# First attention: scores as three products of rounded parts, the query factor moved into the exponential's scale

## The reference

```python
q = rms_norm(einsum('btd,ndh->btnh', x, q_kernel), q_norm_scale)    # 16 heads of 128
k = rms_norm(einsum('bsd,kdh->bskh', x, kv_kernel[0]), k_norm_scale) # 8 heads of 128
q, k = apply_rope(q, positions), apply_rope(k, positions)
logits = einsum('btkgh,bskh->bkgts', q * ATTN_SCALE, k)  # each key head serves two query heads
probs = softmax(where((j <= i) & (i - j < 128), logits, min))
out = einsum(probs, v) @ out_kernel
```

## Time and profile before

| | |
|---|---|
| median of 3 runs | 1593.5 us (1591.81 to 1593.52) |
| profiled execution, own time | 1587.25 us |
| span of its trace | 1585.4 us |
| busy: PE, DVE, ACT, POOL | 93%, 68%, 56%, 25% |
| first attention | the first 656 us or so of the span |
| mean granted TensorE clock | 0.976 of full speed |

### The profile page before, as it was taken

How to read it: one execution, slowest core, us unless ns; L and a number is a source line. 1 busy time by engine, 2 the same in 40 slices (tenths; PEclk the granted TensorE clock), 3 DMA queues, 4 the chain that set the end, 5 groups by cost and what they waited for, 6 DMA issues and landing times.

```text
span 1585.4 us, 24036 instructions
## 1 busy us (share of the span) xinstructions
PE 1478.0 (93%) x7582; PEld 1095.0 (69%) x7582; DVE 1085.6 (68%) x2404; ACT 882.6 (56%) x2052; POOL 403.2 (25%) x473
## 2 busy tenths in 40 slices
PE   4899999999998999799999999999879999999898
PEld 3788788878887888667777777777644444444476
DVE  6898699859976998377555455455438676767654
ACT  4777677757785777444332332332236565756556
POOL 4666566566655665200000000000000000000000
PEclk9999999999999999899999999999969899999999
DMA  6000000000000000233000000000030000000001
GB/s 236 1 1 1 1 1 1 1 3 1 1 1 3 1 1 1 66 91 90 20 1 1 0 0 0 0 0 0 2 135 1 1 1 0 0 0 0 1 14 40
DMA packets 15767, 28.54 MB, mean 18 GB/s; under 512 B 2000, under 2 KB 10064, under 8 KB 15024
## 3 DMA queue, kind: packets, MB, share of 16 engines
q1 hardware_dynamic: 15264, 26.51, 4.9%
q0 software_dynamic: 400, 0.78, 0.3%
HBM read 25.96 MB, written 2.10 MB: 18 GB/s over the span
## 4 chain that ended last, share of the span: by engine, by line
PE 73%; DVE 10%; issue 6%; POOL 5%; ACT 4%; DMA 1%; DVEq 0%; SPq 0%; ACTq 0%; POOLq 0%
PE ps L1126 13%; PE ps L1128 13%; PE ps L1127 13%; PE ps L1396 5%; PE ps L1179 5%; PE ps L1455 4%; PE ps L1225 4%; PE ps L1240 2%; PE ps L1377 2%; POOL rope L388 2%; PE ps L1523 2%; PE ps L1206 2%; DVE ssum L528 1%; PE ps L1281 1%; PE ps L1409 1%
## 5 line engine op out<-in xcount | busy, mean ns | idle before, releaser
L360 POOL TENSOR_TENSOR ln_rs<-ln_ve,minus_half 128x4 f32<-128x4 f32 x16 | 17.4, 1085 | 887.5 <-DVE ln_ve L424 887.5
L710 DVE TENSOR_REDUCE nm<-ps 128x1 f32<-128x512 f32 x256 | 168.3, 687 | 70.2 <-PE ps L1396 68.4
L1126 PE MATMUL ps<-xnT_lo,w1moe_hi 128*128 128x512 f32 x400 | 177.4, 444 | 2.4 <-DVE w2moe_lo L665 2.2
L1044 ACT ACTIVATE pT<-ps 128x512 f32<-128x512 f32 x256 | 143.5, 601 | 62.6 <-PE ps L1409 60.2
L960 ACT ACTIVATE moe_act_hi<-sg 128x512 fp32r<-128x512 f32 x100 | 63.3, 633 | 190.6 <-DVE sg L642 190.6
L1127 PE MATMUL ps<-xnT_hi,w1moe_lo 128*128 128x512 f32 x400 | 160.5, 401 | 0.0
L1128 PE MATMUL ps<-xnT_hi,w1moe_hi 128*128 128x512 f32 x400 | 159.9, 400 | 0.0
L388 POOL TENSOR_TENSOR rope<-rope 128x384 f32<-128x384 f32 x128 | 144.2, 1127 | 0.0
L632 DVE TENSOR_TENSOR sg<-ps,sg 128x512 f32<-128x512 f32 x100 | 69.1, 691 | 96.0 <-ACT sg L980 96.0
L892 ACT ACTIVATE raw<-ps 128x512 f32<-128x512 f32 x128 | 76.4, 597 | 99.3 <-PE ps L1128 97.0
L912 ACT ACTIVATE prob<-ps,nmax 128x256 f32<-128x256 f32 (+1 forms) x256 | 113.2, 457 | 30.8 <-DVE nmax L503 30.7
(11 more groups left out here) (204 smaller groups left out, 3747.3 us busy)
## 6 DMA issues: line engine op xcount, KB each, us to landing
yT<-in_w1moe SPq DMA_DIRECT2D x25, 256.0 KB, 2.6
encT<-in_wqkv SPq DMA_DIRECT2D x8, 512.0 KB, 8.7
w_in<-in_w2moe SPq DMA_DIRECT2D x25, 128.0 KB, 2.7
wo<-in_wo SPq DMA_DIRECT2D x1, 2048.0 KB, 19.1
wm<-in_wm SPq DMA_DIRECT2D x2, 1024.0 KB, 11.9
out_x<-x_res SPq DMA_DIRECT2D x4, 512.0 KB, 2.9
x_res<-in_x SPq DMA_DIRECT2D x1, 1536.0 KB, 14.7
pT<-in_c_pick SPq DMA_DIRECT2D x1, 1024.0 KB, 5.6
```

Of the source, the lines that this page charges most:

```text
L710: V.tensor_reduce(nm1[:, m % 2, t, col:col + 1], ps[:, 2 + i % 2, :], AX.X, ALU.max, negate=True).then_inc(s1_max, 1)
L1044: A(pT1[:, u % 2, 2 * (m % 2) + h, c, :], ps[:, 4 + e % 2, :], ACT.Exp, scale=SCALE1).then_inc(p1_ready, 1)
L1126: MM(out, left[0], right[1], start=first, stop=False)
```

## The change

- The queries are no longer multiplied by their factor. The transposes take the rotated queries directly from `rope1`; only the key is multiplied on DVE (`kn`, 128 columns in place of 384).
- The turned q, q, k are rounded on ACT (two copies, `qT0[0]` and `kT0[0]`, for the one of L900), and DVE subtracts them from the PSUM bank to get the low parts (two instructions more). `qkT_ready` is now signalled by DVE.
- Each head's scores are three fp32r matmuls over both key tiles at once (256 columns, 128 in a group's first tile), six per step, in place of four fp32 products (two in a group's first tile).
- The query factor goes into the exponential: `scale=rms`, and the bias is `nmax` times `rms`, one tiny DVE instruction more, behind a wait for `nmax`.
- Epsilon stands as a 129th column beside the squares, so L528 sums it in and POOL's addition L383 goes. `rms` gets a ring of 6.
- DVE's order in a tick: scale probabilities (n-6), maximum and its product (n-4), key product (n-1), low parts (n-2), sum of squares and rotation (n).

```diff
 # GpSimd
                     pool.wait_ge(summed, k + 1)
-                    if n >= 2:
-                        pool.wait_ge(qk_normed, k - 1)
-                    nc.gpsimd.tensor_tensor(msq[:, s, :], ssum[:, s, :], eps_sum[:], ALU.add).then_inc(meaned, 1)
-                    pool.wait_ge(meaned, k + 1)
-                    nc.gpsimd.tensor_tensor(rms[:, s, :], msq[:, s, :], minus_half[:, 0:3],
+                    if n >= RMS_RING:
+                        pool.wait_ge(prob_ready, k - RMS_RING + 1)
+                        pool.wait_ge(qk_normed, k - RMS_RING + 1)
+                    nc.gpsimd.tensor_tensor(rms[:, n % RMS_RING, :], ssum[:, s, :], minus_half[:, 0:3],
                                             ALU.pow).then_inc(rms_ready, 1)
                     pool.wait_ge(roped, k + 1)
...
 # VectorE
                     dve.wait_ge(scored, k + 1)
+                    if m >= 2:
+                        dve.wait_ge(prob_ready, k - 1)
                     V.tensor_reduce(nmax[:, s, :], ps[:, 3 + s, :].rearrange("p (h f) -> p h f", h=2)[:, :, 0:w],
-                                    AX.X, ALU.max, negate=True).then_inc(max_ready, 1)
+                                    AX.X, ALU.max, negate=True).then_inc(maxed, 1)
+                    dve.wait_ge(maxed, k + 1)
+                    V.tensor_tensor(nshift[:, s, :], nmax[:, s, :], rms[:, m % RMS_RING, 0:2], ALU.mult
+                                    ).then_inc(max_ready, 1)
...
-                    V.tensor_tensor(qkn[:, s, :].rearrange("p (h f) -> p h f", h=3),
-                                    rope1[:, s, :].rearrange("p (h f) -> p h f", h=3),
-                                    rms[:, s, :].unsqueeze(2).to_broadcast((P, 3, P)), ALU.mult
+                    V.tensor_scalar(kn[:, s, :], rope1[:, s, 2 * P:3 * P], rms[:, m % RMS_RING, 2:3], None, ALU.mult
                                     ).then_inc(qk_normed, 1)
+                if new and 2 <= n < STEPS + 2:
+                    m = n - 2
+                    dve.wait_ge(qkT_high, k0 + m + 1)
+                    bank = 5 if m < EARLY_TURNS else 2
+                    V.tensor_tensor(qT0[1][:, m % 2, :, :], ps[:, bank, 0:2 * P].rearrange("p (h f) -> p h f", h=2),
+                                    qT0[0][:, m % 2, :, :], ALU.subtract)
+                    V.tensor_tensor(kT0[1][:, m % QK_RING, :], ps[:, bank, 2 * P:3 * P], kT0[0][:, m % QK_RING, :],
+                                    ALU.subtract).then_inc(qkT_ready, 1)
                 if new and n < STEPS:
                     dve.wait_ge(squared, k + 1)
                     if n >= 2:
-                        dve.wait_ge(rotated, k - 1)
-                        dve.wait_ge(qk_normed, k - 1)
+                        dve.wait_ge(rms_ready, k - 1)
+                        dve.wait_ge(qk_turned, k - 1)
...
 # ScalarE
-                    A(qkT[:, m % QK_RING, :, :], ps[:, 5 if m < EARLY_TURNS else 2, 0:3 * P].rearrange("p (h f) -> p h f", h=3), ACT.Copy
-                      ).then_inc(qkT_ready, 1)
+                    A(qT0[0][:, m % 2, :, :], ps[:, bank, 0:2 * P].rearrange("p (h f) -> p h f", h=2), ACT.Copy)
+                    A(kT0[0][:, m % QK_RING, :], ps[:, bank, 2 * P:3 * P], ACT.Copy).then_inc(qkT_high, 1)
...
-                                bias=nmax[:, s, h:h + 1], accum_out=psums[:, s, h:h + 1])
+                                bias=nshift[:, s, h:h + 1], scale=rms[:, m % RMS_RING, h:h + 1], accum_out=psums[:, s, h:h + 1])
...
 # TensorE
-                        ins = T(ps[:, 5 if m < EARLY_TURNS else 2, h * P:(h + 1) * P], qkn[:, m % 2, h * P:(h + 1) * P], ident[:])
+                        turned = rope1[:, m % 2, h * P:(h + 1) * P] if h < 2 else kn[:, m % 2, :]
+                        ins = T(ps[:, 5 if m < EARLY_TURNS else 2, h * P:(h + 1) * P], turned, ident[:])
...
                     for h in range(2):
-                        for part in ((1,) if t == 0 else (0, 1)):
-                            at = 0 if t == 0 else part * P
-                            ins = MM(bank[:, h, at:at + P], qkT[:, m % QK_RING, h, :],
-                                     qkT[:, (m - 1 + part) % QK_RING, 2, :], start=False,
-                                     stop=h == 1 and part == 1, skip_group_check=True)
+                        for left, right in ((0, 1), (1, 0), (0, 0)):
+                            ins = MM(bank[:, h, 0:w], qT0[left][:, m % 2, h, :],
+                                     kT0[right][:, keys, :].rearrange("p t f -> p (t f)"),
+                                     start=False, stop=h == 1 and left == right, skip_group_check=True)
```

More of the change, by code:

```diff
@@ L33 @@
 STEPS = GROUPS * TT
-RAW_RING, QK_RING, PROB_RING = 9, 4, 3
+RAW_RING, QK_RING, PROB_RING, RMS_RING = 9, 4, 3, 6
+SQ = P + 1
 LAST_LAG = 8
@@ L93, in build @@
         minus_half = sb("minus_half", [P, 16])
-        eps_sum = sb("eps_sum", [P, 3])
         spare = sb("spare", [P, 2])
@@ L107, in build @@
         ssum = sb("ssum", [P, 2, 3], where=part_a)
-        msq = sb("msq", [P, 2, 3], where=part_a)
-        rms = sb("rms", [P, 2, 3], where=part_a)
-        qkT = sb("qkT", [P, QK_RING, 3, P], where=part_a)
+        rms = sb("rms", [P, RMS_RING, 3], where=part_a)
+        qT0 = [sb(f"qT0_{part}", [P, 2, 2, P], F32R, part_a) for part in ("hi", "lo")]
+        kT0 = [sb(f"kT0_{part}", [P, QK_RING, P], F32R, part_a) for part in ("hi", "lo")]
         nmax = sb("nmax", [P, 2, 2], where=part_a)
+        nshift = sb("nshift", [P, 2, 2], where=part_a)
         psums = sb("psums", [P, 2, 2], where=part_a)
@@ L117, in build @@
         rope1 = sb("rope1", [P, 2, 3 * P], where=part_a)
-        rope2 = sb("rope2", [P, 2, 3 * P], where=part_a)
-        qkn = sb("qkn", [P, 2, 3 * P], where=part_a)
+        rope2 = sb("rope2", [P, 2, 3, SQ], where=part_a)
+        kn = sb("kn", [P, 2, P], where=part_a)
         odd_head = [sb(f"odd_head_{part}", [P, SEQ], F32R, part_a) for part in ("hi", "lo")]
@@ L224, in build @@
         projected, raw_kept, squared = sem("projected"), sem("raw_kept"), sem("squared")
-        summed, meaned, rms_ready = sem("summed"), sem("meaned"), sem("rms_ready")
+        summed, rms_ready = sem("summed"), sem("rms_ready")
         roped, rotated, qk_normed = sem("roped"), sem("rotated"), sem("qk_normed")
-        qk_turned, qkT_ready = sem("qk_turned"), sem("qkT_ready")
+        qk_turned, qkT_high, qkT_ready = sem("qk_turned"), sem("qkT_high"), sem("qkT_ready")
         scored, max_ready, prob_ready = sem("scored"), sem("max_ready"), sem("prob_ready")
+        maxed = sem("maxed")
         inv_ready, probn_ready = sem("inv_ready"), sem("probn_ready")
@@ L533, in attention_step @@
                     rh = r3.rearrange("p (h f) -> p h f", h=3)
-                    o2 = rope2[:, s, :].rearrange("p (h f) -> p h f", h=3)
+                    o2 = rope2[:, s, :, 0:P]
                     V.tensor_tensor(o2[:, :, 0:H2], rh[:, :, H2:HD0], sin3[:, t, :, 0:H2], ALU.mult)
@@ L894, in attention_step @@
                         act.wait_ge(rotated, k - 1)
-                    A(sq[:, s, :], ps[:, s, 0:3 * P], ACT.Square).then_inc(squared, 1)
+                    A(sq[:, s, :, 0:P], ps[:, s, 0:3 * P].rearrange("p (h f) -> p h f", h=3), ACT.Square).then_inc(squared, 1)
                 if new and 2 <= n < STEPS + 2:
@@ L1221, in attention_step @@
                            start=True, stop=False, skip_group_check=True)
+                    j = m % QK_RING
+                    keys = slice(j, j + 1) if t == 0 else slice(j - 1, j + 1)
+                    w = P if t == 0 else 2 * P
                     for h in range(2):
-                        for part in ((1,) if t == 0 else (0, 1)):
-                            at = 0 if t == 0 else part * P
-                            ins = MM(bank[:, h, at:at + P], qkT[:, m % QK_RING, h, :],
-                                     qkT[:, (m - 1 + part) % QK_RING, 2, :], start=False,
-                                     stop=h == 1 and part == 1, skip_group_check=True)
+                        for left, right in ((0, 1), (1, 0), (0, 0)):
+                            ins = MM(bank[:, h, 0:w], qT0[left][:, m % 2, h, :],
+                                     kT0[right][:, keys, :].rearrange("p t f -> p (t f)"),
+                                     start=False, stop=h == 1 and left == right, skip_group_check=True)
                     ins.then_inc(scored, 1)
```

8 lines of the change are left out of this document (4 added, 4 removed).

## The result

The changed kernel takes **1673.4 us** (median of 4 runs, 1671.88 to 1673.58), against 1592.85 for the kernel before beside it: a ratio of 1.0511, 95% interval [1.049, 1.0533], 80.5 us slower. The forecast was 1655.5 and its range ended at 1671. The sign and the main mechanism came as predicted, the size did not.

A forecast was written before the change was run, and what follows sets the result against it. PE bounds the kernel before, DVE close behind; the change makes DVE the bound through POOL's hold. +62 us on the profiled 1587.25 gives 1649, plus 6.25 to the median 1655.5; range 1602 to 1671.

The forecast's parts named there:

- S: End of DVE's sum of squares L528 in a step, the zero point from which the prediction counts start times.
- the hold of 0.79: Scaling pair on DVE: POOL's addition L388 delays the maximum L503, 0.79 us lost in every full step.
- DVE's cycle of 4.64: Full step on DVE, one sum of squares to the next: 4.64 us, 4.55 on average, so DVE bounds.
- The 25 intervals: Steps 4 to 29 of a batch: 116.1 us against 100.55 with the norm, +15.5 a batch, 62 for four.
- batch 0's +2: Batch 0's first ticks, DVE-bound by the split weights already: 6 ticks at about +0.4 us, +2.
- The -2: Ticks without projection or rotation, outside the 25 intervals: PE stays the bound, gaining some 0.5 us a batch.
- the +62 of the sum: Whole kernel: four batches at +15.5 us, with +2 and -2 elsewhere, added to the profiled 1587.25 for 1649.
- PE's price of the scores: Scores on PE: six fp32r matmuls 0.68 us, gaining 0.21 in three steps of four, +0.23 in a group's first tile.
- (b): Rival at L388's start: the scaling pair isn't held, PE remains the bound at 14.9 us a group, 1584; 14%.
- (a): Rival at the scaling pair: DVE keeps POOL out of both L495, the key product waits for L388; 1606; 12%.
- (c): Rival: as forecast, but L388 is 0.15 us slower or six 128-column matmuls cost 0.233 and more; 1670; 10%.
- (d): Rival for the whole kernel: gains and losses cancel; 4%.

## Why the prediction was right, and where it was wrong

- **POOL's addition would start 0.02 ahead of the first scaling, and the second would be held in any case: the size right, the place not.** L389 starts at S + 1.30, not S + 1.23, 0.05 behind the first scaling. It is the first that is held and the second that runs free behind it. For DVE's cycle that comes to the same: L507 was put at S + 2.57 and starts at S + 2.54; the hold of 0.79 measures 4.63 - 3.93 = 0.70 against the kernel with epsilon's addition back. The Trainium skill (SBUF — State Buffer, "SBUF: two separate sides") has whoever starts first keeping the pair for the whole instruction. The runs agree with the hold for the whole instruction. Who is first can't be read off the starts of the profile when these are 0.05 us apart: POOL's addition 0.05 behind a first scaling held it in 92 cases of 92, in the changed kernel and again in the kernel before without epsilon's addition; 0.05 behind a second scaling it held it in none of 69, in the kernel before and again in the one with epsilon's addition back.
- **DVE's cycle of 4.64, four steps 18.2: right**, 4.63 and 18.23.
- **The 25 intervals, +15.5 a batch: right, somewhat low.** 117.13 against a predicted 116.1; +66.8 over four batches against 62.
- **"Ticks without a projection or a rotation, outside this stretch, keep PE as the bound and gain some 0.5 a batch, -2": this is the step that failed.** With batch 0's +2 the places outside the 25 intervals were to cancel; they cost 1.6 + 11.1 + 3.1 + 3.8 = 19.6 us less 0.1. Batch 0's term measured +0.9. The -2 measured +11.1 in the last two intervals alone, and up to +6.9 in joints and tail. Where DVE is the bound it arrives at the end of the batch late: the transposes of steps 29, 30 and 31 come 3.9 and 4.3 apart, though no projection stands between them, for PE waits 0.88 and 1.45 for the scaling of six steps earlier (L1257 at 336.60 and 341.27); before, PE waited for nothing there and they came 2.63 and 2.74 apart. In the kernel with the short addition, where DVE is just about on time, the same two intervals still cost 3.4 in all. The joints (+0.9, +1.7, +0.4) and 2.1 of the tail, up to the end of the attention, fit the same lateness, but no run isolates it there. Two parts of the 19.6 are not the change's, as far as the traces tell: 1.7 of the tail lies behind the attention, and the kernel before with the norm spread, which changes nothing there either, has the same 1.7; and batch 2's first four steps (15.27 for 14.37) follow a stretch at granted clock 0.50, 371.8 to 375.2, while in the changed kernel with the norm spread, at 1.00 there, they take 14.29. That leaves some 17. Of the 24.3 us between the +62 of the sum and the 86.3 of the traces, 19.5 lie in these places and 4.8 in the 25 intervals.
- **"I expect no change of it" (the granted clock): wrong in the norm's tick of two batches**, and small. The scaling comes so late there that PE waits 2.07 us, and in batches 2 and 3 the matmuls behind that wait start 0.43 apart instead of 0.23:

```profile
445.91 0.65 PE L1257 MATMUL ps<-ident,prob 128*128 128x128 f32 x4 [2.07 <-DVE prob L497]
...
448.49 0.63 PE L1142 MATMUL ps<-wqkv_hi,xnT_hi 128*128 128x512 f32 x1
448.92 0.63 PE L1140 MATMUL ps<-wqkv_lo,xnT_hi 128*128 128x512 f32 x1
```

  That is the lower of the two levels, 1.2 GHz, granted for 3.4 us. The same wait of 2.07 stands in batches 0 and 1 with no fall behind it, so the wait alone doesn't decide. It costs 0.7 and 0.8 us in all in the two batches, since DVE bounds the steps behind it and hides the rest.
- **PE's price of the scores: right and worth nothing.** Six matmuls of 256 columns start 0.118 apart (0.113 taken), those of 128 columns 0.112 (0.113 taken, between 0.111 and 0.233). It gains PE 0.2 in three steps of four. Nowhere here did it become time: even without the hold four steps take 15.27, about before's 15.31. That was the weak joint of rival (b), which gave PE's 14.9: with the hold away the changed kernel takes 1597, 5 over the kernel before.
- **The 6.25 us added because the profiled execution lay under the median:** the changed kernel's lies 0.2 above its own median. The sum of +62 on 1587.25 gave 1649 and the profiled execution took 1673.56; the offset happened to hide a quarter of the miss.
- **Rivals.** (a) needs undisturbed scalings and a key product that waits for POOL; the pair takes 1.37. The key product does wait for POOL in the first steps of a batch: in nine places, 7.5 us, and in the kernel with epsilon's addition back in 12 places, 10.2 us. (b) is the kernel with the short addition. (c) is out: the addition with its three-part pattern takes 0.91 in the step above and 0.999 in the mean of 128, where 1.0 was taken, and the matmuls cost what was taken; its 1670 came nearest by accident. (d) did not happen.

What stays open: whether the fp32r scores could gain once DVE has real slack, about 0.3 us in four steps, an estimate from PE's prices (three times 0.18 gained, 0.22 lost once). No run here had it. Open too is what decides between the two engines when their rows start within 0.05 us, and what makes the clock fall behind one wait of 2.07 us and not behind another.

## What to carry to other kernels

Where two engines exclude each other, ask of every edit where the start of the long instruction of the one moves against the sensitive instructions of the other: taking an instruction off an idle engine cost 34 us here, and putting it back gained 53. A row that merges two instructions hides which of them is held, so ask for each alone. Shortening or splitting work on the busy engine can create such a meeting as well, so check the start times on both timelines, not the busy shares. And when a change turns the bound to another engine, price the ends of the pipeline and the joints between batches too: the lateness gathered in the steady part was paid there again, some 17 us of 86.

## What the runs showed of the hardware that was not expected

- Raising three columns to the power -1/2 on POOL (L386) lasts 1.23 us (mean 1233 ns over 128), where the same instruction behind epsilon's addition took 0.91. It now starts 0.05 us behind DVE's first rotation product, which reads two SBUF tensors; in the kernel before without epsilon's addition it lasts 1.23 too, and with the addition put back 0.91. DVE's product keeps its 0.56. That it starts after idle time isn't the reason: of the kernel before's powers of four columns (L360), which also start after idle time, those beside a DVE instruction with two SBUF inputs (L804) last 1.4 us and those beside one that reads PSUM (L642) 1.0. So POOL pays as well when DVE is first, 0.3 us here, and it is this that put L389 at S + 1.30: the prediction had L386 end at S + 1.00, and it ends at S + 1.32.
- DVE's two-column product of two SBUF inputs is held for 0.24 us by a POOL instruction that started 0.02 us earlier (the rows of the kernel with maximum first and key product on POOL).
- Instructions of DVE that read PSUM are not held: the low part (0.42) and the maximum (0.68) run with POOL's addition beside them, in the timeline of the kernel with the maximum first.
